# Who spreads k over two heads: from three ScalarE reads to one, and a 0/1 factor on VectorE

## The chip, the cores and the metric

One NeuronCore of one Trainium2 chip runs the whole kernel. The metric is the device time of one launch in microseconds. Before the change it is 622.71 us, the median of 3 runs (622.13 to 622.75).

## The reference

A transformer layer with adaptive normalisation, on x of shape 8 x 512 x 256 (batch, tokens, channels), fp32. With six rows of modulation per batch it computes

```
h = layernorm(x) * (1 + ca) + sa
x = x + ga * attention_block(h)     # 16 heads of 16 channels, causal band of 128 keys,
                                    # then an MLP 256 -> 1024 -> 256 with gelu
h = layernorm(x) * (1 + cb) + sb
x = x + gb * channel_mix(h)         # token shift, receptance, squared relu
```

Inside the attention block, `q = h @ Wq + bq`, `k = h @ Wk + bk`, `v = h @ Wv + bv`, `softmax(q k^T / 4 + band) v`, and an output projection. What is changed here is only how the projected k, with its bias, reaches the layout in which the scores are computed.

## The kernel before

Every engine has its own hand-written order of calls; semaphores join them. The work of attention is cut into 16 units: unit `u` is one batch (`u // 2`) and one half of the heads (8 heads, 128 channels on the 128 partitions). Each unit runs through

- `project(u)` (TensorE): q and k, each [128 channels x 512 tokens], into two of the four PSUM banks of `ring_s`, a ring in which each bank is handed on when its last reader signals. The calls that follow on TensorE are `context(u-2)` (one bank of `ring_s` for the denominators) and then `scores` (two pieces of two matmuls each, one bank a piece). So the second piece of scores takes the bank in which q lay, and waits for its last reader, `s_ql`, and the third piece takes k's.
- `high_qk(u)` (ScalarE) and `low_qk(u)` (VectorE): every value is split into a rounded fp16 part (high) and the fp16 rest (low), because the matmuls run in fp16 and add three products. q goes into `q_two` [128, high/low, 512].
- k goes into `k_two` [128, high/low, 1024]: each token has two adjacent columns, one for the even head of a pair and one for the odd. `pick` [128, 2] holds 1.0 where the partition belongs to that head and 0.0 elsewhere, so in each of the two columns the other head's channels are zero. Column `a` of all tokens is a write with a step of two elements.
- `stacks(u, ...)` (SyncE's queue): DMAs from `q_two` and `k_two` into the layout of `scores`, after `s_ql` and `s_kl`.
- `maxima(u, 0..3)` (TensorE, then VectorE L1527 and L1530): row maxima from the high parts alone; it waits for `s_kh`.

The lines of the profile that matter: L958 is ScalarE's high part of q; L961 its high part of k, once for each column, with scale `pick` and bias `bias_k`; L964 its fp32 copy of k into `kc`. L1513 is VectorE's low part of q from PSUM, L1517 its low part of k from `kc`, once for each column. L983 is ScalarE's copy of the denominators of an earlier unit (`copy_den`), L1480 VectorE's `scale_x`, L1611 `residual_b`, L1562 `residual_a`. On GpSimd, L2174 to L2179 are `select` (the causal band), L2189 and L2191 `sums`, L2218 `scale_y`, L2209 `bias_x`. L342 are the matmuls of `scores`, L361 those of `context`, L307 those of `maxima`. Around `high_qk` ScalarE's order has `copy_den` and `exps` behind it; around `low_qk` VectorE's has `residual_b` (even u from 8) or `scale_x` (odd u) behind it.

In the main part of the kernel a batch, two units, takes 67 us, and its pattern repeats. "Unit 10" is the unit whose q is read at 317 us, "unit 11" the one at 350 us.

Of the kernel before, what the change touches and what calls it, by code (L numbers as in the profile page):

```python
# [8 lines left out]
F16 = mybir.dt.float16  # L9
# [5 lines left out]
P = 128  # L15
# [26 lines left out]
def adaln_block(nc, x, w_attn, w_ff1, w_ff2, w_mix, w_mod, c_t, cols, bo, b2, out):  # L42
# [22 lines left out]
    with ctx:  # L65
# [21 lines left out]
        bias_k = sb("bias_k", [P, 2, 2])  # L87
# [54 lines left out]
        kc = sb("kc", [P, L])  # L142
# [25 lines left out]
        s_qk, s_qh, s_ql, s_kc, s_kh, s_kl = (sem(n) for n in ("qk", "qh", "ql", "kc_s", "kh", "kl"))  # L168
# [21 lines left out]
        s_bm, s_bq, s_cv, s_ro, s_row, s_pick, s_bk = (sem(n) for n in ("bm", "bq_s", "cv_s", "ro", "row_s", "pick_s", "bk"))  # L190
# [17 lines left out]
        squares_v = kc[:, :].rearrange("p (k n) -> p k n", k=KC)  # L208
# [21 lines left out]
        def _(e):  # L230
# [23 lines left out]
            def project(u):  # L254
# [3 lines left out]
                for i in range(2):  # L258
                    c0 = i * D + half * P
                    bank, free = ring_s.take(("qk", u, i), *((s_ql, u + 1), (s_kc, u + 1))[i])  # L260
# [509 lines left out]
            for b in range(3, 7):  # L770
                u = 2 * b
                gp = 8 * b
                scores(gp - 1, 0, 2)
                values(b, 1)
                down(u - 4, 0)
                maxima(u, 3)
                keys(u - 5)
                transposes_b(u - 3)
                max_rows(u)
                scores(gp - 1, 2, 4)  # L780
                project(u + 1)
                context(u - 1)
                scores(gp, 0, 2)
                receptance(u - 5)
                scores(gp, 2, 4)
                scores(gp + 1, 0, 2)
                down(u - 4, 1)
                scores(gp + 1, 2, 4)
                scores(gp + 2, 0, 2)
                values_b(u - 5)  # L790
                up(u - 3, 0, 1)
                maxima(u + 1, 0)
                up(u - 3, 1, 2)
                maxima(u + 1, 1)
                up(u - 3, 2, 3)
                up(u - 3, 3, 4)
                out_project(u - 2)
                maxima(u + 1, 2)
                down(u - 3, 0)
                scores(gp + 2, 2, 4)  # L800
                transposes_d(u - 4)
                scores(gp + 3, 0, 2)
                transposes_a(b + 1)
                down(u - 3, 1)
                maxima(u + 1, 3)
                keys(u - 4)
                scores(gp + 3, 2, 4)
                max_rows(u + 1)
                project(u + 2)
                context(u)  # L810
                scores(gp + 4, 0, 2)
                scores(gp + 4, 2, 4)
                transposes_b(u - 2)
                scores(gp + 5, 0, 2)
                receptance(u - 4)
                maxima(u + 2, 0)
                up(u - 2, 0, 1)
                maxima(u + 2, 1)
                up(u - 2, 1, 2)
                out_project(u - 1)  # L820
                scores(gp + 5, 2, 4)
                scores(gp + 6, 0, 2)
                transposes_d(u - 3)
                scores(gp + 6, 2, 4)
                values_b(u - 4)
                maxima(u + 2, 2)
                up(u - 2, 2, 3)
                up(u - 2, 3, 4)
                values(b + 1, 0)

            scores(NG - 9, 0, 2)
            values(B - 1, 1)
            down(10, 0)
            maxima(NU - 2, 3)
            keys(9)
            transposes_b(11)
            max_rows(NU - 2)
            scores(NG - 9, 2, 4)
            project(NU - 1)
            context(NU - 3)  # L840
            scores(NG - 8, 0, 2)
            scores(NG - 8, 2, 4)
            receptance(9)
            scores(NG - 7, 0, 2)
            scores(NG - 7, 2, 4)
            down(10, 1)
            maxima(NU - 1, 0)
            values_b(9)
            up(11, 0, 1)
            maxima(NU - 1, 1)  # L850
            up(11, 1, 2)
            scores(NG - 6, 0, 2)
            out_project(NU - 4)
            up(11, 2, 3)
            maxima(NU - 1, 2)
            up(11, 3, 4)
            maxima(NU - 1, 3)
            down(11, 0)
            transposes_d(10)
            scores(NG - 6, 2, 4)  # L860
            max_rows(NU - 1)
            down(11, 1)
            scores(NG - 5, 0, 2)
            scores(NG - 5, 2, 4)
            transposes_b(NU - 4)
            receptance(10)
            scores(NG - 4, 0, 2)
            scores(NG - 4, 2, 4)
            keys(10)
            out_project(NU - 3)  # L870
            scores(NG - 3, 0, 2)
            values_b(10)
            scores(NG - 3, 2, 4)
            scores(NG - 2, 0, 2)
            up(NU - 4, 0, 1)
            up(NU - 4, 1, 2)
            context(NU - 2)
            up(NU - 4, 2, 3)
            scores(NG - 2, 2, 4)
            up(NU - 4, 3, 4)  # L880
            scores(NG - 1, 0, 2)
            down(NU - 4, 0)
            transposes_b(NU - 3)
            transposes_d(11)
            scores(NG - 1, 2, 4)
            down(NU - 4, 1)
            up(NU - 3, 0, 1)
            up(NU - 3, 1, 2)
            context(NU - 1)
# [3 lines left out]
            transposes_d(NU - 4)  # L893
            up(NU - 3, 2, 3)
            up(NU - 3, 3, 4)
            out_project(NU - 2)
            down(NU - 3, 0)
            keys(NU - 4)
            down(NU - 3, 1)
            transposes_b(NU - 2)  # L900
            receptance(NU - 4)
            up(NU - 2, 0, 1)
            up(NU - 2, 1, 2)
            out_project(NU - 1)
            up(NU - 2, 2, 3)
            values_b(NU - 4)
            up(NU - 2, 3, 4)
            transposes_b(NU - 1)
            down(NU - 2, 0)
            transposes_d(NU - 3)  # L910
            up(NU - 1, 0, 1)
            down(NU - 2, 1)
            up(NU - 1, 1, 2)
            up(NU - 1, 2, 3)
            keys(NU - 3)
            receptance(NU - 3)
            values_b(NU - 3)
            up(NU - 1, 3, 4)
            transposes_d(NU - 2)
            down(NU - 1, 0)  # L920
            down(NU - 1, 1)
            keys(NU - 2)
            receptance(NU - 2)
            values_b(NU - 2)
            transposes_d(NU - 1)
            warm_end(0, 16)
            keys(NU - 1)
            receptance(NU - 1)
            values_b(NU - 1)

        @block.scalar
        def _(e):
# [14 lines left out]
            def high_qk(u):  # L947
# [3 lines left out]
                if u == 0:  # L951
                    e.wait_ge(s_bk, 2)
# [1540 lines left out]
        def _(e):  # L2493
# [57 lines left out]
            def load_residual(i):  # L2551
# [5 lines left out]
                if i == 1:  # L2557
                    e.wait_ge(s_gates, DMA)
# [218 lines left out]
```

## Time and profile before

| | |
|---|---|
| timed runs | 622.71 us median (622.13 to 622.75) |
| the profiled execution | span 620.5 us from first to last instruction; no further time of its own is recorded |
| TensorE | matmuls busy 567.8 us, 92% |
| ScalarE | busy 446.9 us, 72% |
| VectorE | busy 403.2 us, 65% |
| GpSimd | busy 380.3 us, 61% |
| TensorE's clock | mean granted 0.989 of full speed |

The span is 2.2 us below the median of the timed runs. Times in the rows below count from the span's start. A busy TensorE is not TensorE at its peak; what counts for the change is at which instruction a wait ends last.

### The profile page before, as it was taken

The page shows a single profiled execution, that of the slowest core. Times are in us where ns is not written, and L with a number is a line of the kernel's source. Part 1 is how long each engine was busy: PE and PEld are TensorE (multiplying, and loading weights), DVE is VectorE, ACT ScalarE, POOL GpSimd, SP SyncE. Part 2 cuts the span into 40 slices and gives each one's busy share as a digit, 9 for nine tenths or more (in the row PEclk, how much of TensorE's full clock was granted, in tenths as well). Part 3 has the DMA queues.
Part 4 walks back from the last instruction along what each step waited for, and adds up shares of the span by engine and source line. Part 5 has one row for each costly group of instructions (what it writes and reads, how often), then busy time and mean ns, then how long its engine had stood idle before and what let it go on. Part 6 is the DMA issues. An engine that isn't in the chain of part 4 may idle for free.

```text
span 620.5 us, 16499 instructions
## 1 busy us (share of the span) xinstructions
PE 567.8 (92%) x6528; PEld 444.8 (72%) x6528; DVE 403.2 (65%) x830; ACT 446.9 (72%) x745; POOL 380.3 (61%) x610
## 2 busy tenths in 40 slices
PE   5889988999898999999898989899999989999996
PEld 2668757777776777677667767677767768878785
DVE  4676746686464788576867686578867475375453
ACT  2527447499968777897879786987788798955542
POOL 4387324657937957675767678586657378943430
PEclk9989989899999999999999999999999999999999
DMA  5635423434503051351235132533134242110111
GB/s 176 246 103 133 124 77 78 112 75 116 137 18 101 25 139 52 97 143 56 69 90 153 60 87 76 146 93 89 52 80 112 70 116 52 54 46 26 34 44 35
DMA packets 46364, 55.74 MB, mean 90 GB/s; under 512 B 11643, under 2 KB 33469, under 8 KB 46286
## 3 DMA queue, kind: packets, MB, share of 16 engines
q1 hardware_dynamic: 44454, 53.81, 31.4%
q8 instruction: 52, 0.85, 0.6%
q10 hardware_dynamic: 1832, 0.87, 0.6%
q14 instruction: 26, 0.21, 0.1%
HBM read 22.31 MB, written 4.49 MB: 43 GB/s over the span
## 4 chain that ended last, share of the span: by engine, by line
PE 50%; ACT 17%; DVE 15%; issue 7%; POOL 7%; DMA 1%; SPq 1%; ACTq 1%; DVEq 0%; POOLq 0%
PE rest L486 4%; PE rest L498 4%; PE rest L447 3%; PE rest L449 3%; PE rest L448 3%; DVE nmax L1530 3%; PE quad L342 3%; ACT rest L1048 3%; PE rest L361 3%; PE rest L474 3%; PE rest L239 3%; PE quad L398 2%; ACT hid_hi L1058 2%; ACT p L997 2%; DVE hid_lo L1590 2%
## 5 line engine op out<-in xcount | busy, mean ns | idle before, releaser
L2174 POOL TENSOR_SCALAR_AFFINE_SELECT p<-p 128x448 f32<-128x448 f32 x64 | 41.5, 649 | 102.8 <-ACT p L997 80.5
L1530 DVE TENSOR_REDUCE nmax<-quad 128x8 f32<-128x1032 f32 x64 | 79.0, 1234 | 2.2
L430 PE MATMUL rest<-bt_hi,w_hi 128*128 128x256 f16 x256 | 70.2, 274 | 5.3 <-DVE hid_lo L1590 5.1
L997 ACT ACTIVATE p<-quad,scale_s 128x576 f32<-128x576 f32 (+1 forms) x77 | 62.3, 822 | 15.7 <-PE quad L342 15.4
L1048 ACT ACTIVATE rest<-rest,bias,scale_g 128x256 f32<-128x256 f32 x128 | 63.0, 532 | 11.2 <-PE rest L432 11.0
L447 PE MATMUL rest<-w_hi,hid_hi 128*128 128x256 f16 x256 | 69.9, 273 | 0.9 <-DVE hid_lo L1590 0.9
L432 PE MATMUL rest<-bt_hi,w_lo 128*128 128x256 f16 x256 | 69.8, 273 | 0.0
L431 PE MATMUL rest<-bt_lo,w_hi 128*128 128x256 f16 x256 | 69.8, 273 | 0.0
L449 PE MATMUL rest<-w_hi,hid_lo 128*128 128x256 f16 x256 | 69.8, 272 | 0.0
L448 PE MATMUL rest<-w_lo,hid_hi 128*128 128x256 f16 x256 | 69.8, 272 | 0.0
L1590 DVE SCALAR_TENSOR_TENSOR hid_lo<-rest,inv_f,hid_hi 128x512 f16<-128x512 f32 x64 | 46.8, 744 | 25.1 <-ACT hid_hi L1058 24.8
L2189 POOL TENSOR_TENSOR ps<-p 128x384 f32<-128x384 f32 x56 | 56.7, 1012 | 1.4
L2191 POOL TENSOR_TENSOR ps<-ps,p 128x320 f32<-128x320 f32 x56 | 49.1, 877 | 4.4
L342 PE MATMUL quad<-q_st,k_st 100*128 100x192 f16 (+3 forms) x468 | 45.1, 228 | 6.8 <-DVE x L1562 2.7
L1058 ACT ACTIVATE hid_hi<-rest,inv_f 128x512 f16<-128x512 f32 x64 | 43.4, 687 | 4.5 <-PE rest L449 2.2
L342 PEld LDWEIGHTS quad<-q_st,k_st 100*128 100x128 f16 x468 | 33.1, 97 | 16.7 <-issue 3.7
L1527 DVE COPY_PREDICATED quad<-later,quad 128x248 f32<-128x248 int16 x64 | 26.8, 418 | 28.2 <-PE quad L307 28.1
L361 PE MATMUL rest<-p,v_blk 128*32 128x192 f32 (+2 forms) x1024 | 41.2, 314 | 0.9 <-POOL p L2179 0.9
L361 PEld LDWEIGHTS rest<-p,v_blk 128*32 128x32 f32 x1024 | 31.9, 112 | 12.8 <-issue 5.8
L239 PE MATMUL rest<-ident 128*128 128x128 f32 x292 | 41.1, 292 | 0.0
L239 PEld LDWEIGHTS rest<-ident 128*128 128x128 f32 x292 | 37.1, 202 | 1.8 <-issue 0.7
L1517 DVE SCALAR_TENSOR_TENSOR k_two<-kc,pick,k_two 128x512 f16<-128x512 f32 x32 | 24.7, 827 | 20.1 <-ACT kc L964 20.1
(239 smaller groups left out, 1531.9 us busy)
## 6 DMA issues: line engine op xcount, KB each, us to landing
k_st<-k_two SPq DMA_DIRECT2D x64, 128.0 KB, 2.5
v_blk<-vn SPq DMA_DIRECT2D x16, 512.0 KB, 6.4
q_st<-q_two SPq DMA_DIRECT2D x64, 64.0 KB, 2.6
k_st<-k_two SPq DMA_DIRECT2D x64, 64.0 KB, 2.0
rb<-den_rows SPq DMA_DIRECT2D x16, 256.0 KB
x<-x SPq DMA_DIRECT2D x16, 256.0 KB, 3.0
out<-x SPq DMA_DIRECT2D x16, 256.0 KB, 2.2
xa<-x SPq DMA_DIRECT2D x7, 512.0 KB, 4.8
```

The costliest lines, as they stand in the source:

```text
L239: e.matmul(psum[4 if n < WARM else 7 if n < WARM + 5 else 5][:, 0:P], ident[:, :], ident[:, :], start=True, stop=True)
L342: last = e.matmul(bank[:, c0:c0 + w], k_st[0:MR, half, j, s * P:(s + 1) * P], q_st[0:MR, half, j, s * KW + q0:s * KW + q0 + w], start=True ...
L361: e.matmul(bank[32 * j:32 * j + 32, s * KW:s * KW + w], v_blk[:, s % 2, s // 2, half, 2 * j * HD:2 * (j + 1) * HD], p32[(4 * u + j) % SLOT ...
L430: e.matmul(dst, w1_hi[:, k, ms], bt_hi[:, k, :], start=(k == 0), stop=False)
L431: e.matmul(dst, w1_hi[:, k, ms], bt_lo[:, k, :], start=False, stop=False)
L432: last = e.matmul(dst, w1_lo[:, k, ms], bt_hi[:, k, :], start=False, stop=(k == KC - 1))
L447: e.matmul(dst, hid_hi[:, m, ts], w2_hi[:, m, :], start=(m == 0), stop=False)
L448: e.matmul(dst, hid_hi[:, m, ts], w2_lo[:, m, :], start=False, stop=False)
L449: last = e.matmul(dst, hid_lo[:, m, ts], w2_hi[:, m, :], start=False, stop=(m == MF - 1))
L997: e.activation(p32[gp % SLOTS][:, c0:c0 + 2 * w].rearrange("p (n c) -> p n c", n=2), (rest if gp < APART else quad)[:, b0 % HQ:b0 % HQ + 2 ...
L1048: e.activation(dst, dst, ACT.Gelu_apprx_tanh, bias=bias_1[:, m:m + 1], scale=scale_g[:, 0:1]).then_inc(s_gl, 1)
L1530: e.tensor_reduce(nmax[:, :, :, qt].rearrange("p a j -> p j a"), quad[:, :, 2 * QB - 2:2 * WIN].rearrange("p j (c a) -> p j a c", a=2), AX ...
```

## The change

ScalarE reads the projected k once and writes it rounded to fp16 into the new dense tile `k_one[:, 0, :]`, in place of two scaled reads into `k_two` and one fp32 copy into `kc`. VectorE multiplies that tile by `pick`, once for each column, into the high half of `k_two`; subtracts it from the PSUM value plus bias into `k_one[:, 1, :]`, the low part; does q's low part; and multiplies k's low part by `pick`, twice. `bias_k` and its two small instructions go. The PSUM bank of k is handed on at `s_ko`, after VectorE's read, in place of `s_kc`.

```
 high_qk (ScalarE)
-                    e.wait_ge(s_bk, 2)
+                    e.wait_ge(s_bq, 2)
...
-                kt_hi = k_two[m][:, 0, :]
                 e.activation(q_two[m][:, 0, :], ring_s.at["qk", u, 0][:, :], ACT.Identity, bias=bias_q[:, 2 * m:2 * m + 1]).then_inc(s_qh, 1)
                 e.wait_ge(s_qk, 2 * u + 2)
-                for a in range(2):
-                    e.activation(kt_hi[:, a:2 * L:2], ring_s.at["qk", u, 1][:, :], ACT.Identity, bias=bias_k[:, m, a:a + 1],
-                                 scale=pick[:, a:a + 1]).then_inc(s_kh, 1)
                 hold(e, s_kl, 2 * u)
-                e.activation(kc[:, :], ring_s.at["qk", u, 1][:, :], ACT.Identity, bias=bias_q[:, 2 * m + 1:2 * m + 2]).then_inc(s_kc, 1)
+                e.activation(k_one[:, 0, :], ring_s.at["qk", u, 1][:, :], ACT.Identity, bias=bias_q[:, 2 * m + 1:2 * m + 2]).then_inc(s_kc, 1)
 low_qk (VectorE)
-                e.wait_ge(s_qh, u + 1)
+                if u == 0:
+                    e.wait_ge(s_pick, 1)
+                e.wait_ge(s_kc, u + 1)
+                for a in range(2):
+                    e.tensor_scalar(kt_hi[:, a:2 * L:2], k_one[:, 0, :], pick[:, a:a + 1], None, ALU.mult).then_inc(s_kh, 1)
+                e.scalar_tensor_tensor(out=k_one[:, 1, :], in0=ring_s.at["qk", u, 1][:, :], scalar=bias_q[:, m + 1:m + 2],
+                                       in1=k_one[:, 0, :], op0=ALU.add, op1=ALU.subtract).then_inc(s_ko, 1)
                 e.scalar_tensor_tensor(out=qt_lo[:, :], in0=ring_s.at["qk", u, 0][:, :], scalar=bias_q[:, m:m + 1],
                                        in1=qt_hi[:, :], op0=ALU.add, op1=ALU.subtract).then_inc(s_ql, 1)
-                e.wait_ge(s_kc, u + 1)
+                e.wait_ge(s_ko, u + 1)
                 for a in range(2):
-                    e.scalar_tensor_tensor(out=kt_lo[:, a:2 * L:2], in0=kc[:, :], scalar=pick[:, a:a + 1],
-                                           in1=kt_hi[:, a:2 * L:2], op0=ALU.mult, op1=ALU.subtract).then_inc(s_kl, 1)
+                    e.tensor_scalar(kt_lo[:, a:2 * L:2], k_one[:, 1, :], pick[:, a:a + 1], None, ALU.mult).then_inc(s_kl, 1)
```

The diff has three more kinds of lines. The loops over batches in the five orders are written out call by call; the sequence of calls on every engine is the same as before. Some waits are added: `hold(e, s_xve, n)`, `hold(e, s_hve, n)`, `hold(e, s_bve, i)` and `hold(e, s_cve, i)` ahead of VectorE's four kinds of statistics, each for a small GpSimd instruction of the batch or half batch before, `hold(e, s_h2, 4 * n)` ahead of GpSimd's `rstd_x(n)`, and at one place each `s_hn` and `s_top`. And the scratch of a setup step lies in `h3` instead of `kc`.

## Rows read from the trace of the kernel before

**Rows 1.** The page: busy us of each engine; GpSimd's select (busy, mean ns).

```profile
PE 567.8 (92%) x6528; PEld 444.8 (72%) x6528; DVE 403.2 (65%) x830; ACT 446.9 (72%) x745; POOL 380.3 (61%) x610
...
L2174 POOL TENSOR_SCALAR_AFFINE_SELECT p<-p 128x448 f32<-128x448 f32 x64 | 41.5, 649 | 102.8 <-ACT p L997 80.5
```

**Rows 2.** Chain that ended last, 317 to 352 us: start, us, what.

```profile
317.96 1.68 ACT k_two L961 x2
...
332.10 0.69 DVE x L1562
...
332.84 0.34 PE quad L342 x2
```

**Rows 3.** Waits of TensorE, 230 to 506 us: total us, times, longest.

```profile
PE quad L342 <- DVE x L1562: 2.7, 4, 0.7
```

**Rows 4.** Timeline of ScalarE, units 10 and 11: start, us, line, [idle before].

```profile
317.91 1.74 ACT L961 ACTIVATE k_two<-quad,bias_k,pick 128x512 f16<-128x512 f32 x2
...
319.49 0.68 ACT L964 ACTIVATE kc<-quad,bias_q 128x512 f32<-128x512 f32 x1
...
321.44 0.60 ACT L983 ACTIVATE dn<-quad 128x512 f32<-128x512 f32 x1
...
349.88 0.68 ACT L958 ACTIVATE q_two<-quad,bias_q 128x512 f16<-128x512 f32 x1
...
353.54 0.60 ACT L983 ACTIVATE dn<-quad 128x512 f32<-128x512 f32 x1 [0.83 <-PE quad L381]
```

**Rows 5.** Timeline of VectorE, the same two units.

```profile
320.20 1.68 DVE L1517 SCALAR_TENSOR_TENSOR k_two<-kc,pick,k_two 128x512 f16<-128x512 f32 x2 [1.46 <-ACT kc L964]
...
321.77 0.68 DVE L1611 TENSOR_TENSOR x<-x 128x512 f32<-128x512 f32 x1
...
352.74 1.48 DVE L1517 SCALAR_TENSOR_TENSOR k_two<-kc,pick,k_two 128x512 f16<-128x512 f32 x2 [1.39 <-ACT kc L964]
...
354.12 1.26 DVE L1480 SCALAR_TENSOR_TENSOR h<-xa,mv_x,mod_a 128x256 f32<-128x256 f32 x3
```

**Rows 6.** VectorE's groups by line and shape, whole span.

```profile
L1517 DVE SCALAR_TENSOR_TENSOR k_two<-kc,pick,k_two 128x512 f16<-128x512 f32 x32 | 24.7, 827 | 20.1 <-ACT kc L964 20.1
...
L1513 DVE SCALAR_TENSOR_TENSOR q_two<-quad,bias_q,q_two 128x512 f16<-128x512 f32 x16 | 11.9, 746 | 22.3 <-ACT q_two L958 22.3
...
L1480 DVE SCALAR_TENSOR_TENSOR h<-xa,mv_x,mod_a 128x256 f32<-128x256 f32 x28 | 11.6, 477 | 0.3
```

**Rows 7.** Timeline of GpSimd, the same two units.

```profile
318.47 0.88 POOL L2191 TENSOR_TENSOR ps<-ps,p 128x320 f32<-128x320 f32 x1
...
319.31 1.29 POOL L2218 TENSOR_TENSOR x<-x,mod_g 128x512 f32<-128x512 f32 x1
...
350.67 0.88 POOL L2191 TENSOR_TENSOR ps<-ps,p 128x320 f32<-128x320 f32 x1
...
351.55 1.29 POOL L2209 TENSOR_TENSOR x<-x,row_b 128x512 f32<-128x512 f32 x1
```

**Rows 8.** Timeline, VectorE and GpSimd, at 168 us and at 141 us.

```profile
168.55 0.86 POOL L2191 TENSOR_TENSOR ps<-ps,p 128x320 f32<-128x320 f32 x1
...
169.12 0.84 DVE L1611 TENSOR_TENSOR x<-x 128x512 f32<-128x512 f32 x1
...
169.37 1.05 POOL L2174 TENSOR_SCALAR_AFFINE_SELECT p<-p 128x448 f32<-128x448 f32 x1
...
140.86 2.69 DVE L1489 SCALAR_TENSOR_TENSOR h<-h,rs_x,mod_a 128x256 f32<-128x256 f32 x4
```

**Rows 9.** Timeline of TensorE, the first scores of unit 11.

```profile
353.40 0.50 PE L342 MATMUL quad<-q_st,k_st 100*128 100x192 f16 x4
```

**Rows 10.** Timeline of VectorE, unit 2.

```profile
67.14 0.72 DVE L1513 SCALAR_TENSOR_TENSOR q_two<-quad,bias_q,q_two 128x512 f16<-128x512 f32 x1
...
69.13 0.14 DVE L1693 TENSOR_REDUCE total<-rest 128x1 f32<-128x2 f32 x1
```

**Rows 11.** Waits of TensorE, 107 to 158 us.

```profile
PE quad L342 <- DVE nmax L1530: 0.6, 2, 0.4
```

More of the change, by code:

```diff
@@ new lines, in _ @@
+            values(4, 0)
+            scores(31, 0, 2)
+            values(4, 1)
+            down(4, 0)
+            maxima(8, 3)
+            keys(3)
+            transposes_b(5)
+            max_rows(8)
+            scores(31, 2, 4)
+            project(9)
+            context(7)
+            scores(32, 0, 2)
+            receptance(3)
+            scores(32, 2, 4)
+            scores(33, 0, 2)
+            down(4, 1)
+            scores(33, 2, 4)
+            scores(34, 0, 2)
+            values_b(3)
@@ new lines, in _ @@
+            stats_b(4)
+            output(1)
+            low_a(4)
+            mix(2)
+            maxima(7, 3)
+            add_y(3)
+            low_m(7)
+            low_qk(8)
+            residual_b(3)
+            divide(6)
+            low_b(4)
+            maxima(8, 0)
+            maxima(8, 1)
+            low_f(4, 0, 1)
+            low_f(4, 1, 2)
+            residual_a(5)
+            gated(2)
+            maxima(8, 2)
+            stats_x(5)
+            output(2)
+            stats_b(5)
@@ new lines, in _ @@
+            low_f(4, 2, 3)
+            low_f(4, 3, 4)
+            mix(3)
+            maxima(8, 3)
+            scale_c(6)
+            low_m(8)
+            low_qk(9)
+            scale_x(5)
+            low_b(5)
+            divide(7)
+            shift_x(5)
+            stats_h(5)
+            gated(3)
+            add_y(4)
+            maxima(9, 0)
+            low_f(5, 0, 1)
+            scale_c(7)
+            low_f(5, 1, 2)
+            maxima(9, 1)
+            residual_b(4)
+            residual_a(6)
@@ new lines, in _ @@
+            low_f(5, 2, 3)
+            low_f(5, 3, 4)
+            maxima(9, 2)
+            stats_b(6)
+            output(3)
+            low_a(5)
+            mix(4)
+            maxima(9, 3)
+            add_y(5)
+            low_m(9)
+            low_qk(10)
+            residual_b(5)
+            divide(8)
+            low_b(6)
+            maxima(10, 0)
+            maxima(10, 1)
+            low_f(6, 0, 1)
+            low_f(6, 1, 2)
+            residual_a(7)
+            gated(4)
+            maxima(10, 2)
@@ new lines, in _ @@
+            maxima(11, 1)
+            residual_b(6)
+            residual_a(8)
+            low_f(7, 2, 3)
+            low_f(7, 3, 4)
+            maxima(11, 2)
+            stats_b(8)
+            output(5)
+            low_a(6)
+            mix(6)
+            maxima(11, 3)
+            add_y(7)
+            low_m(11)
+            low_qk(12)
+            residual_b(7)
+            divide(10)
+            low_b(8)
+            maxima(12, 0)
+            maxima(12, 1)
+            low_f(8, 0, 1)
@@ new lines, in _ @@
+            residual_a(15)
+            stats_b(15)
+            low_f(14, 2, 3)
+            gated(12)
+            low_f(14, 3, 4)
+            low_b(15)
+            output(12)
+            mix(13)
+            add_y(14)
+            low_f(15, 0, 1)
+            low_f(15, 1, 2)
+            low_f(15, 2, 3)
+            residual_b(14)
+            gated(13)
+            output(13)
+            low_f(15, 3, 4)
+            mix(14)
+            add_y(15)
+            scale_y(15)
+            residual_b(15)
@@ L2412, in _ @@
+            bias_x(9)
+            select(48)
+            rstd_h(7)
+            bias_h(13)
+            select(49)
+            sums(48)
             scale_y(8)
@@ L2475, in _ @@
[L2475 to L2491 removed]
+            rstd_b(13)
```

1535 lines of the change are left out of this document (966 added, 569 removed).

## The prediction

> **What bounds the kernel now.** I read the page first. TensorE is busy 92% of the span, ScalarE 72%, VectorE 65%, GpSimd 61% [rows 1]. So at most 8% of the span, some 50 us, is there to win, and engine time that is freed elsewhere counts only where a wait of TensorE ends later because of it. Next the chain that ended last: in unit 10 it runs through exactly the work that is changed, ScalarE's two scaled reads of k, then its fp32 copy, VectorE's low parts, `residual_b`, its statistics, the gelu, and `residual_a` (L1562), and comes back to TensorE as a wait of scores [rows 2]. That wait occurs 4 times between 230 and 506 us, 2.7 us in all [rows 3]: units 8, 10, 12 and 14. The odd units between are not on it. Then the timelines of the two units, engine by engine: what stands behind the changed calls, and when TensorE asks.
>
> **ScalarE's side.** Removed: two reads (1.74 us together) and the copy (0.68) [rows 4]; added: one read to dense fp16, by q's own row 0.68. That is 1.7 us of ScalarE per unit, 28 us over 16 units. Most of it shortens no wait. In unit 11, `copy_den` comes next and ScalarE already idles 0.83 us for `context` [rows 4]; in unit 10 two squares follow and then `copy_den` at 321.44, which is when `context` ends too. Finishing earlier makes that idle time longer. I find only units 4 and 5 (119 to 152 us) in which ScalarE goes from the copy straight on for several microseconds. There TensorE's own waits are small: the one for the row maxima that follow is 0.6 us in two times [rows 11]. I take 0.6 us gained; 0 if it is covered again, 3.1 us (two times the 1.55 us by which ScalarE's next call can move up) if all of it comes through.
>
> **VectorE's side.** Before: one q instruction (0.746 us) and two for k (0.827) [rows 6]. After: the same q instruction, one of its shape for k's low part, and four multiplications of a 16-bit tile by a column. Consecutive instructions overlap by 0.11 us (320.20 + 1.68 against 321.77 [rows 5]), so a q-like instruction costs 0.65 us from start to start.
>
> The multiplication is not in this trace: no wide VectorE instruction has one source only, in SBUF, 16 bits wide. Upper end: L1517 with the same strided output, 0.69 us from start to start ((354.12 - 352.74) / 2 [rows 5]). Lower end: two elements a cycle, which would be the 0.39 us of a 256-column instruction ((1.26 - 0.477) / 2 [rows 5, 6]). I take 0.39: every wide row at one element a cycle has a second tensor or a PSUM source, and this has neither. The Trainium skill (VectorE: DVE Perf Modes, section "Mode 2×_2P") says that `tensor_scalar` between SBUF tiles takes two read ports and gives two results a cycle; that would be the low end, and no row here shows it.
>
> Unit 10, by 0.39: the k read runs 317.91 to 318.60, VectorE starts 0.03 later at 318.63 (as 320.17 to 320.20 [rows 4, 5]). Four multiplications and two q-like instructions end at 318.63 + 1.56 + 1.30 = 321.49; the next call started at 321.77. A gain of 0.28 us. By 0.69 it is 322.69, a loss of 0.92. The break-even is 0.46 us a multiplication: VectorE's wait for the copy (1.46 us) used to stand where the new work goes.
>
> **What runs beside them.** GpSimd is in the middle of a row of two-source instructions just when the first two multiplications come: `sums` to 319.35, `scale_y` to 320.60; in unit 11 to 351.55 and 352.84 [rows 7]. Before, VectorE ran q's low part there, which has one SBUF source. At 169.12 a VectorE instruction that reads two SBUF tiles meets a GpSimd one with 0.29 us to go and takes 0.84 us in place of 0.68 (321.77 [rows 5]); the GpSimd instruction behind it takes 1.05 us against a mean of 0.649 [rows 1, 8]. Four more at 140.86 take 2.69 us [rows 8], about 1 us more than L1480's pace. So the two engines do make each other wait, by turns. If a multiplication does so too, the first loses 0.72 - 0.13 = 0.59 us, `scale_y` gets its turn and ends near 320.80, the second loses 1.06, and the next call starts at 323.14: a loss of 1.37 in unit 10. If not, the gain of 0.28 stays. Both ends are open; I take the middle, a loss of 0.55 in each of four units: 2.2 us.
>
> **The bank of q.** This is the new wait. `s_ql` comes behind three more instructions, and the second piece of scores takes that bank. In unit 11 TensorE starts its four matmuls at 353.40 and needs the bank at about 353.6 [rows 9]. ScalarE's k read starts right behind q's (349.88 + 0.68 [rows 4], less 0.10 of overlap: 350.46) and ends at 351.15; VectorE starts at 351.18; q's low part is done at 351.18 + 0.78 + 0.65 + 0.75 = 353.36: 0.2 us to spare. With 0.69 a multiplication it is 353.96, 0.4 us late. With turns: 0.24 lost to `sums`, 1.10 to `bias_x`, done at 354.70, 1.14 us late. The middle of 0 and 1.14 is 0.57, in five odd units (7 to 15): 2.9 us. Nothing takes this back: TensorE is in order, and behind it stand scores, `receptance` and the MLP. VectorE's own next call, 354.12, is hidden by its later wait for TensorE unless it slips by more than 1 us. Even units have more time, since TensorE's `context` starts later against q.
>
> **Unit 2.** Here VectorE comes late and ScalarE has finished: q, k and k took 69.13 - 67.14 = 1.99 us [rows 10]. Now 4 x 0.39 + 2 x 0.65 = 2.86: a loss of 0.9 us, and maxima and `scale_x` behind it are on the chain. With 0.69 it is 2.1.
>
> **Costed at nothing.** `k_two`'s DMAs start later behind other work in SyncE's queue in units 10 and 11 and have idle time behind them. `s_kh` is out before `maxima` asks in both units. The added holds are for GpSimd instructions of the batch or half batch before; uncovered, each would cost the wait for one small instruction. Written-out loops issue the same calls. `bias_k` and the scratch in `h3` touch setup only.
>
> **Sum.** 2.2 + 2.9 + 0.9 - 0.6 = 5.4 us on a span of 620.5, so 625.9; the timed median lies 2.2 us above the span, so 622.7 + 5.4 = 628.1 us.
>
> **Rivals.**
> 1. Each multiplication runs at one element a cycle and waits for nobody. For: it costs what every wide row costs. Against: it has neither of their reasons. 4 x 0.92 + 5 x 0.4 + 2.1 - 0.6 = 7.2: 629.9 us. Chance 0.18.
> 2. They run fast and undisturbed. For: L1517 too reads two SBUF tiles, and its mean is only 0.827 us. Against: [rows 8]. -4 x 0.28 + 0 + 0.9 - 0.6 = -0.8: 621.9 us. Chance 0.21.
> 3. Faster: as 2, and ScalarE's freed time comes through wholly in units 4 and 5, where its calls stand back to back. It decides if TensorE's waits there shrink by more than 1 us. -1.1 + 0.9 - 3.1 = -3.3: 619.4 us. For: ScalarE is the busiest after TensorE. Against: [rows 11]. Chance 0.16.
> 4. Full turns: both multiplications for the high part wait out the whole GpSimd instruction in front, in all nine units. 4 x 1.37 + 5 x 1.14 + 0.9 - 0.6 = 11.5: 634.2 us. For: the row at 169.12. Against: it needs GpSimd to win between two adjacent VectorE instructions each time. Chance 0.10.
>
> The rule beside rival 4 is the Trainium skill's, SBUF — State Buffer, section "Who interferes with whom": VectorE in a two-port mode and GpSimd exclude each other for a whole instruction. By that rule, the trace agrees for instructions with two SBUF sources (0.16 us at 169.12).
>
> My own case, 624 to 632 us, has the remaining 0.35.
>
> **Chances and range.** About 0.2% (1.2 us) is what a measurement here can tell from no change. Faster: rival 3 and a fifth of rival 2, 0.20. Same: the rest of 2, 0.17. Slower: the forecast, rivals 1 and 4, 0.63. The range goes from 620.0, between rivals 2 and 3, to 634.0; outside lie most of rival 3 below and half of rival 4 above, under 0.2. Both signs hold much of the chance, so the forecast's own range is 624 to 632.
>
> **What will show it.** Right: a multiplication of about 0.4 us alone and up to 1.5 us beside `sums`, `scale_y` and `bias_x`; a new wait of L342 for VectorE's `q_two` in odd units; ScalarE busy 28 us less with more idle before L983; and no shorter wait for L1562. Wrong: multiplications at 0.4 us throughout, or at 0.78, or the waits between 107 and 158 us gone. The weakest step is how long the first two multiplications last.

## The result, and the profile after

The changed kernel takes 635.52 us (median of 4 runs, 634.47 to 640.64), the kernel before, timed beside it, 622.73 us (4 runs, 622.13 to 624.51). The ratio is 1.0222, 95% interval 1.0184 to 1.0259: slower by 12.8 us. The forecast was 628.1 us with a range of 620.0 to 634.0, so the sign is right and the time lies outside the range, next to rival 4 (634.2). The profiled execution took 634.47 us with a span of 632.4, which is 11.9 us more than the span before; it is the shortest of the four after, and the one before is a middle one, which is why the spans stand 11.9 apart and the medians 12.8.

The page after, busy us of each engine, against [rows 1]:

```profile
PE 566.7 (90%) x6528; PEld 442.6 (70%) x6528; DVE 427.4 (68%) x876; ACT 423.0 (67%) x713; POOL 382.5 (60%) x610
```

ScalarE has 23.9 us less work (28 were forecast; the durations added up there overlap by about 0.1 us each) and VectorE 24.2 us more. TensorE does the same work in a longer span. VectorE's groups after, by line and shape (busy us, mean ns | idle before and for whom), against [rows 6]:

```profile
L1847 DVE TENSOR_SCALAR k_two<-k_one,pick 128x512 f16<-128x512 f16 x32 | 27.6, 917 | 32.1 <-ACT k_one L1126 32.1
L1854 DVE TENSOR_SCALAR k_two<-k_one,pick 128x512 f16<-128x512 f16 x32 | 15.0, 520 | 0.0
L1850 DVE SCALAR_TENSOR_TENSOR q_two<-quad,bias_q,q_two 128x512 f16<-128x512 f32 x16 | 11.8, 737 | 0.0
L1848 DVE SCALAR_TENSOR_TENSOR k_one<-quad,bias_q,k_one 128x512 f16<-128x512 f32 x16 | 11.7, 732 | 0.0
```

L1847 and L1854 are the same instruction on the same shapes, the first for k's high part, the second for its low part. One takes 917 ns in the mean and the other 520. What differs is what stands beside them. VectorE's timeline of unit 10 (start, us, line, [idle before]), and GpSimd's under it, against [rows 5] and [rows 7]:

```profile
324.54 2.46 DVE L1847 TENSOR_SCALAR k_two<-k_one,pick 128x512 f16<-128x512 f16 x2 [2.22 <-ACT k_one L1126]
326.90 0.73 DVE L1848 SCALAR_TENSOR_TENSOR k_one<-quad,bias_q,k_one 128x512 f16<-128x512 f32 x1
327.55 0.73 DVE L1850 SCALAR_TENSOR_TENSOR q_two<-quad,bias_q,q_two 128x512 f16<-128x512 f32 x1
328.21 0.90 DVE L1854 TENSOR_SCALAR k_two<-k_one,pick 128x512 f16<-128x512 f16 x2
329.00 0.67 DVE L1948 TENSOR_TENSOR x<-x 128x512 f32<-128x512 f32 x1
```

```profile
324.38 0.87 POOL L2614 TENSOR_TENSOR ps<-ps,p 128x320 f32<-128x320 f32 x1
325.20 1.48 POOL L2641 TENSOR_TENSOR x<-x,mod_g 128x512 f32<-128x512 f32 x1
```

The low pair takes 329.00 - 328.21 = 0.79 us from start to start, 0.39 an instruction, the forecast's own figure. The high pair takes 326.90 - 324.54 = 2.36, 1.57 us more, and ends only when `scale_y` has ended at 326.68. That is the full turn of rival 4 (0.59 + 1.06 = 1.65 by the prediction). `scale_y` itself takes 1.48 us in place of 1.29 [rows 7]. In unit 11 the pair takes 2.01 us.

What TensorE makes of it: its waits over the span (us in total, times, longest), against [rows 3]:

```profile
PE quad L341 <- DVE q_two L1850: 8.2, 9, 1.3
...
PE quad L341 <- DVE x L1898: 4.2, 4, 1.0
...
PE quad L302 <- DVE q_two L1850: 2.1, 2, 1.4
...
PE quad L373 <- DVE q_two L1850: 1.3, 1, 1.3
```

The first, third and fourth are new: TensorE waits for the bank of q, which q's low part gives back. The first falls in unit 4 and in units 7 to 14, the third in units 1 and 2, the fourth in unit 5. The second was 2.7 us. The chain of waits in unit 11 (start, us, what), which had nothing of the changed work in an odd unit before:

```profile
357.66 0.70 ACT k_one L1126
...
358.38 2.11 DVE k_two L1847 x2
360.49 0.62 DVE k_one L1848
361.12 0.67 DVE q_two L1850
...
361.83 0.34 PE quad L341 x2
```

**Where the 11.9 us lie.** A useful ruler is the start of ScalarE's read of q in each unit; I call the time to the next unit's start the step of a unit. After minus before, the steps are: unit 4 +1.29, unit 5 +1.34, unit 6 0.0; odd units 7, 9, 11 and 13 +1.21, +0.99, +1.05 and +1.10; even units 8, 10, 12 and 14 +1.29, +1.30, +1.28 and +1.27. Unit 4 itself starts 0.20 earlier (118.22 against 118.42), and from unit 15 to the end it is 137.09 against 137.10. The sum is 2.63 + 4.35 + 5.14 - 0.20, or 11.9 us.

The -0.20 is no sign that units 0 to 3 cost nothing. Up to unit 4, TensorE's mean granted clock is 0.94 in the execution before and 0.97 in the one after. Two runs below that leave this work as it was up to there, e4 and e11, have 0.97 too and start unit 4 at 117.19 and 116.00. The step of unit 2 shows it best (start and end, length, busy us of PE, PEld, DVE, ACT and POOL, granted clock, DMA share, GB/s; before, after, e4, e11):

```profile
63.38:91.58 28.20, 26.74 (x357) 19.96 (x355) 17.13 (x44) 12.63 (x18) 6.92 (x15) 0.88 0.32 89
64.27:91.70 27.43, 25.04 (x357) 19.32 (x355) 18.14 (x47) 11.21 (x16) 6.97 (x15) 0.94 0.37 90
65.25:91.19 25.94, 24.97 (x357) 19.42 (x355) 17.13 (x44) 12.62 (x19) 6.71 (x15) 0.93 0.37 97
62.98:89.18 26.20, 25.07 (x357) 19.35 (x355) 17.12 (x44) 12.61 (x18) 6.72 (x15) 0.93 0.35 96
```

At nearly the same clock the step is 1.2 to 1.5 us longer after the change, and up to unit 4 the loss is 1.0 to 2.2 us. These are single executions, so the size is rough.

### The profile page after: what moved, and what is told of

Read it like the earlier page. It is cut to its first block, busy times and chain, and to the rows that moved or that the text cites. A ratio compares the mean times of both kernels' runs of the same rounds, so it can differ in the third digit from the quotient of the medians.

```text
span 632.4 us, 16579 instructions
## 1 busy us (share of the span) xinstructions
PE 566.7 (90%) x6528; PEld 442.6 (70%) x6528; DVE 427.4 (68%) x876; ACT 423.0 (67%) x713; POOL 382.5 (60%) x610
## 4 chain that ended last, share of the span: by engine, by line
PE 46%; DVE 20%; ACT 15%; POOL 9%; issue 7%; DMA 2%; ACTq 1%; SPq 0%; DVEq 0%; POOLq 0%
PE rest L485 4%; DVE k_two L1847 4%; PE rest L497 4%; PE rest L446 3%; PE rest L448 3%; PE rest L447 3%; ACT rest L1210 3%; DVE nmax L1866 3%; PE quad L341 3%; PE rest L473 3%; ACT p L1159 2%; ACT hid_hi L1220 2%; PE quad L397 2%; PE rest L238 2%; DVE hid_lo L1927 2%
## 5 line engine op out<-in xcount | busy, mean ns | idle before, releaser
L1847 DVE TENSOR_SCALAR k_two<-k_one,pick 128x512 f16<-128x512 f16 x32 | 27.6, 917 | 32.1 <-ACT k_one L1126 32.1
L360 PE MATMUL rest<-p,v_blk 128*32 128x192 f32 (+2 forms) x1024 | 39.8, 307 | 0.9 <-POOL p L2602 0.9
L360 PEld LDWEIGHTS rest<-p,v_blk 128*32 128x32 f32 x1024 | 31.3, 110 | 11.9 <-issue 5.8
```

Of the source, the lines that this page charges most:

```text
L360: e.matmul(bank[32 * j:32 * j + 32, s * KW:s * KW + w], v_blk[:, s % 2, s // 2, half, 2 * j * HD:2 * (j + 1) * HD], p32[(4 * u + j) % SLOT ...
```

## The experiments

This table holds what I read from each timeline; it is worked out, not printed by the profile. "q low" and "block" give, counted from the start of ScalarE's read of q, when q's low part ends and when the last of the unit's k and q instructions on VectorE ends (median of four units). Even is units 8 to 14, odd is 7 to 13; us.

```
kernel          start  step   step   even   odd    q low      block
                of 4   of 4   of 5   step   step   even/odd   even/odd
before          118.42 27.21  35.49  32.68  34.24  1.48 1.47  4.61 4.34
after           118.22 28.50  36.83  33.97  35.33  5.09 4.72  5.91 5.55
e1 q first      117.14 28.26  35.33  33.43  34.24  1.47 1.46  5.39 5.03
e2 hi from PSUM 117.84 29.17  36.49  33.13  34.81  4.25 4.20  5.07 5.01
e3 both         119.99 28.93  35.32  32.75  34.50  1.47 1.47  4.58 4.56
e4 holds only   117.19 27.20  35.49  32.94  34.37  1.47 1.47  4.57 4.36
e5 cut, after   117.10 28.05  36.95  32.97  34.36  4.06 3.70  4.88 4.53
e6 cut, before  116.34 26.76  35.50  32.49  34.49  1.47 1.46  4.41 4.36
e7 q low last   125.47 28.81  37.32  33.43  35.65  5.23 5.04  5.23 5.04
e8 hi late      116.83 27.46  35.57  32.87  34.24  1.47 1.46  4.80 4.46
e12 q second    122.78 28.28  36.19  34.1*  34.66  4.42 4.05  6.04 5.66
* units 10 and 12, see there
```

e4 leaves the k and q work as it was, so its distance from the first row is scatter. Its odd steps are 34.23 to 34.49, against 34.24 to 34.35 before, its even ones 32.22 to 33.22, against 32.28 to 32.76. Differences of 0.3 us in a step, and of more in a single even one, are not results.

**e1: q's low part first.** The kernel after, with one instruction back where it was.

```diff
+    e.wait_ge(s_qh, u + 1)
+    e.scalar_tensor_tensor(out=qt_lo, ...).then_inc(s_ql, 1)
     e.wait_ge(s_kc, u + 1)
     for a in range(2): e.tensor_scalar(kt_hi[:, a:2 * L:2], k_one[:, 0, :], ...)
     e.scalar_tensor_tensor(out=k_one[:, 1, :], ...)
-    e.scalar_tensor_tensor(out=qt_lo, ...).then_inc(s_ql, 1)
```

> The changed kernel with q's low part moved in front of the two multiplications of k's high part, so that q's bank is handed on early; nothing else differs. My theory (two costs: the multiplications wait by turns with GpSimd, and q's bank is handed on late): TensorE's waits of L341 for q_two go from 8.2 us to nearly 0, the multiplications still take up to 1.5 us, and what is left is the 0.8 us that units 8, 10, 12 and 14 lose on the chain plus 0.9 us in unit 2: 626 to 628 us against 635.5 for the changed kernel. Rival A (the 24 us of added VectorE work is the cost, in whatever order): no gain from the order, 634 to 636 us. Rival B (the late bank is the whole cost): 622 to 623 us.

Measured: 626.31 us (624.13 to 631.58, 10 runs), ratio 1.0086 [1.0054, 1.0119]. The new wait for `q_two` is gone, and with it the loss of the odd units (34.24, as before) and of unit 5 (35.33). The even units keep +0.75, and unit 4 keeps +1.05. TensorE's waits between 236 and 520 us in this kernel:

```profile
PE quad L341 <- DVE x L1899: 5.7, 4, 1.5
```

So about 9 of the 13 us hang on the place of one instruction. In the even units, what stays sits in the other path, where the scores wait for `residual_a`. In unit 4 it is the other bank: TensorE waits for the read of k's low part, which now frees k's bank (window 117.14 to 145.40 us).

```profile
PE quad L341 <- DVE k_one L1851: 0.9, 1, 0.9
```

**e2: k's high part from PSUM.** The order of the kernel after, but the multiplication reads the bank and not `k_one`, so it has one source in PSUM.

```diff
-    e.tensor_scalar(kt_hi[:, a:2 * L:2], k_one[:, 0, :], pick[:, a:a + 1], None, ALU.mult)
+    e.tensor_scalar(kt_hi[:, a:2 * L:2], ring_s.at["qk", u, 1], bias_q[:, m + 1:m + 2], pick[:, a:a + 1], ALU.add, ALU.mult)
```

> The changed kernel with the two multiplications of k's high part reading the projected k from PSUM (add bias, times pick, rounded on the way out) instead of the dense SBUF tile; same order. My theory: an instruction that reads PSUM does not wait for GpSimd, so each takes 0.73 to 0.75 us always (now 0.481 to 1.572 us, mean 0.917), GpSimd's scale_y returns to 1.28 us, and per unit the loss falls to 0.3 us on the chain and 0.3 us for the bank, 1.4 us in unit 2: 626 to 628 us. Rival A (added VectorE work is the cost): 32 instructions of 0.74 instead of 0.917 us save 6 us of VectorE's 24, so about a quarter of the loss goes: 632 us. Rival C (the strided 16-bit output makes them slow, not GpSimd): durations stay scattered up to 1.5 us, 635 us.

Measured: 630.92 us (629.61 to 631.41, 4 runs), ratio 1.0141 [1.0107, 1.0175], 3 us above what I expected. The lines of `k_two`'s writers give min/median/max ns; first this kernel, then the kernel after:

```profile
L1847 DVE TENSOR_SCALAR k_two<-quad,bias_q,pick x32: 819/860/882, 27.9 to 492.5; 128x512 f16<-128x512 f32 x32
```

```profile
L1847 DVE TENSOR_SCALAR k_two<-k_one,pick x32: 481/766/1572, 27.9 to 497.5; 128x512 f16<-128x512 f16 x32
L1854 DVE TENSOR_SCALAR k_two<-k_one,pick x32: 494/503/969, 30.1 to 499.6; 128x512 f16<-128x512 f16 x32
```

From PSUM the instruction lasts the same everywhere, with GpSimd beside it or not: the spread of 481 to 1572 ns belongs to the form that reads SBUF. I had put this form at 0.73 to 0.75 us and it is 0.86. q's low part still ends at 4.20 in odd units, and their step is 0.57 longer; units 4 and 5 are 1.96 and 1.00 longer, and the expectation had no term for them.

**e3: both.** q's low part first, then k's high part from PSUM once ScalarE has read the bank.

```diff
+    e.wait_ge(s_qh, u + 1); e.scalar_tensor_tensor(out=qt_lo, ...)
     e.wait_ge(s_kc, u + 1)
-    e.tensor_scalar(kt_hi[:, a:2 * L:2], k_one[:, 0, :], ...)
+    e.tensor_scalar(kt_hi[:, a:2 * L:2], ring_s.at["qk", u, 1], bias_q[:, m + 1:m + 2], ...)
     e.scalar_tensor_tensor(out=k_one[:, 1, :], ...)
-    e.scalar_tensor_tensor(out=qt_lo, ...)
```

> Both edits together: q's low part first, then k's high part from PSUM. My theory: VectorE does q's low part while ScalarE reads k, no turns with GpSimd, so the next VectorE call comes 0.3 us earlier than in the kernel before in units 8, 10, 12 and 14, no wait for q's bank, 1.4 us lost in unit 2: 621 to 624 us, no different from the kernel before or a little faster. Rival A (added VectorE work is the cost): 630 to 633 us.

Measured: 627.01 us (626.67 to 627.43, 4 runs), ratio 1.0081 [1.0049, 1.0113]; a miss. The even steps are back (32.75), and the odd ones nearly: 34.50, a value that odd steps take in e4 and e6 too, where no bank is late. But unit 4 costs 1.72 us more than before: VectorE comes to it late, and k's low part, the last reader of a PSUM bank of the unit, ends 5.42 us after q's read began, where q's low part ended at 3.31 before. TensorE waits for it (window 119.99 to 148.92 us):

```profile
PE quad L341 <- DVE k_one L1852: 1.6, 1, 1.6
```

Another 1.6 us have arisen before unit 4 starts, at a granted clock of 0.96 up to there; what of them is the edit's stays open.

**e4: the added waits alone.** The kernel before, with the added holds and nothing else of the change.

```diff
     e.wait_ge(s_x, DMA * (n + 1))
+    hold(e, s_xve, n)
...
     stats(xa, ...)
...
     e.wait_ge(s_xmv, 4 * (n + 1))
+    hold(e, s_h2, 4 * n)
```

> The kernel before with only the added waits of the change (ahead of VectorE's statistics, GpSimd's rstd_x and one load of SyncE). My theory: they are for work long done, 622.7 us, within 0.2%. Rival D (one of them holds VectorE or GpSimd up and carries part of the 12.8 us): 1 us or more above it.

Measured: 622.43 us (621.03 to 625.08, 10 runs), ratio 1.0011 [0.999, 1.0033]. They cost nothing that can be measured; the interval leaves room for 2 us at most, of the 12.8.

**e5 and e6: GpSimd's neighbours cut short.** In both kernels, after (e5) and before (e6), the multiplication in `scale_y` and the addition in `bias_x` work on 8 of 256 columns. The other columns are left as they are, so this part of the computation is left out. The two are read against each other.

```diff
-    e.tensor_tensor(x1[:, ts, :], x1[:, ts, :], mod_g[:, :]..., ALU.mult)
+    e.tensor_tensor(x1[:, ts, 0:8], x1[:, ts, 0:8], mod_g[:, 0:8]..., ALU.mult)
-    e.tensor_tensor(rows, rows, row_b[:, 1:2, :]..., ALU.add)
+    e.tensor_tensor(rows[:, :, 0:8], rows[:, :, 0:8], row_b[:, 1:2, 0:8]..., ALU.add)
```

> The kernel after with GpSimd's two additions and multiplications of 256 columns a tile, scale_y and bias_x, cut to 8 columns (the other columns are left unscaled, so part of the computation is left out). To be read against the kernel before with the same cut, not against the kernel before itself. If the pair of multiplications is long because the second of them waits out scale_y or bias_x (2.46 us a pair in unit 10, 2.11 in unit 11), the pair falls to some 1.3 us in both, and the two cut kernels stand 12.8 minus 4 x 1.1 minus 5 x 0.9, that is 3 to 5 us, apart. If the loss comes from the order alone (q's low part behind three instructions, its bank released late), the cut changes nothing of it and they stand 11 to 13 us apart.

> The kernel before with the same cut of scale_y and bias_x to 8 columns (part of the computation left out). The mate of the run above. It shortens GpSimd's work, which is off the path that sets the end, and takes waits from VectorE's other instructions: 619 to 622 us by either theory.

Measured: e5 628.35 us (625.38 to 636.21, 9 runs), e6 621.72 us (619.57 to 624.02, 10 runs). They stand 6.6 us apart in place of 12.8 (the profiled spans 5.2). VectorE and GpSimd in unit 10 of e5:

```profile
320.25 1.43 DVE L1847 TENSOR_SCALAR k_two<-k_one,pick 128x512 f16<-128x512 f16 x2 [2.22 <-ACT k_one L1126]
321.58 0.73 DVE L1848 SCALAR_TENSOR_TENSOR k_one<-quad,bias_q,k_one 128x512 f16<-128x512 f32 x1
```

```profile
320.09 0.87 POOL L2614 TENSOR_TENSOR ps<-ps,p 128x320 f32<-128x320 f32 x1
320.92 0.42 POOL L2641 TENSOR_TENSOR x<-x,mod_g 128x16 f32<-128x16 f32 x1
```

The same instructions of VectorE, untouched, take 1.33 us from start to start in place of 2.36, once GpSimd's neighbour is short; nothing else was edited. What is left above 0.79 is the wait for `sums`, 0.54 us. The odd steps fall from +1.09 to nothing (34.36, against 34.49 in e6), although three instructions still stand ahead of q's low part: it ends at 3.70, just in time. So in this kernel neither the order nor the turns cost by themselves in odd units; their sum does. The even steps keep +0.48 against e6, and their block ends 0.47 later. The 6.6 us are more than the 3 to 5 expected. Units 4 and 5, where `scale_y` isn't the neighbour, keep +1.29 and +1.45 (28.05 and 36.95, against 26.76 and 35.50 in e6), and I had not counted them.

**e7: q's low part last, in the kernel before.** No dense k, no multiplication that reads it.

```diff
-    e.wait_ge(s_qh, u + 1); e.scalar_tensor_tensor(out=qt_lo, ...)
     e.wait_ge(s_kc, u + 1)
     for a in range(2): e.scalar_tensor_tensor(out=kt_lo[:, a:2 * L:2], in0=kc, ...)
+    e.wait_ge(s_qh, u + 1); e.scalar_tensor_tensor(out=qt_lo, ...)
```

> The kernel before with one instruction moved: q's low part behind k's two low parts, as late as the change puts it, with no multiplication of the dense k in it. If the late release of q's bank costs by itself (PE's first score matmul of the next unit waits for it), the two low parts ahead of it (1.48 to 1.68 us) put it 1.0 to 1.3 us late in each of nine units: 630 to 634 us. If only the waits by turns with GpSimd cost and the place of q's low part is free: 622 to 624 us. In between, 625 to 629, both count.

Measured: 643.47 us (641.72 to 644.91, 4 runs), ratio 1.0335 [1.0294, 1.0375]: 21 us, far more than expected. I had sized it in nine units. It costs in all: odd steps +1.41, even +0.75, units 4, 5 and 6 +1.6, +1.83 and +1.19, the stretch from unit 15 on +0.75, and unit 4 starts 7.0 us later than before. In units 0 to 3 too q's low part now waits for the fp32 copy, and TensorE waits 2.5 us for it in unit 1; how the 7.0 us divide was not isolated. In odd units this is the bank of q by itself. In even ones the edit also moves the end of the block from 4.61 to 5.23, so there it is both paths. TensorE in unit 11 of e7, start, us, [idle before]:

```profile
369.29 0.34 PE L342 MATMUL quad<-q_st,k_st 100*128 100x192 f16 x2
370.87 0.34 PE L342 MATMUL quad<-q_st,k_st 100*128 100x192 f16 x2 [1.24 <-DVE q_two L1517]
```

**e12: q's low part second, in the kernel after.** Made to test the two paths against each other by a number.

```diff
     for a in range(2): e.tensor_scalar(kt_hi[:, a:2 * L:2], k_one[:, 0, :], ...)
+    e.wait_ge(s_qh, u + 1); e.scalar_tensor_tensor(out=qt_lo, ...)
     e.scalar_tensor_tensor(out=k_one[:, 1, :], ...)
-    e.scalar_tensor_tensor(out=qt_lo, ...)
```

> The kernel after with q's and k's low parts changed about: high multiplications, q's low part, k's low part, low multiplications. Theory of two paths: odd units pay for the end of q's low part beyond 3.65 us after q's high part began (4.70 in the kernel after, so 1.1; here 4.03, so 0.4), even units for the end of the whole block (5.91 against 4.60, so 1.3, here unchanged); units 4 and 5 win at most 0.7 together: 635.5 - 4 x 0.66 - 0.7 = 631 to 633 us. If q's bank sets the even units as well, they win 0.66 each too: 628.5 to 630. If neither, 635.

Measured: 634.33 us (632.51 to 639.33, 6 runs), ratio 1.0202 [1.0165, 1.0239]; three of the runs lie at 632.5 to 633.2, within the 631 to 633 expected, the median 1.3 us above. The steps tell more than the times. Odd: 34.66, +0.42 where +0.4 was expected. Even: units 10 and 12 take 34.02 and 34.17, +1.4. They won nothing although q's low part ends 0.67 us earlier; the block now ends at 6.04 in place of 5.91. (Units 8 and 14 of this execution take 35.82 and 35.27: the granted clock is 0.95 in each, against 1.00 in unit 10.) TensorE's waits in unit 8, the same in unit 10, first of the kernel after, then of e12:

```profile
PE quad L341 <- DVE x L1898: 1.0, 1, 1.0
PE quad L341 <- DVE q_two L1850: 0.8, 1, 0.8
```

```profile
PE quad L341 <- DVE x L1899: 1.8, 1, 1.8
...
PE quad L341 <- DVE k_one L1851: 0.3, 1, 0.3
```

The wait for q's bank goes away and the wait for `residual_a` grows by what it gave: 1.8 us in both.

**e8: both PSUM readers first, the multiplications after them.**

```diff
+    e.wait_ge(s_qh, u + 1); e.scalar_tensor_tensor(out=qt_lo, ...)
     e.wait_ge(s_kc, u + 1)
+    e.scalar_tensor_tensor(out=k_one[:, 1, :], ...)
     for a in range(2): e.tensor_scalar(kt_hi[:, a:2 * L:2], k_one[:, 0, :], ...)
-    e.scalar_tensor_tensor(out=k_one[:, 1, :], ...)
-    e.scalar_tensor_tensor(out=qt_lo, ...)
```

> The kernel after with both low parts that read PSUM (q's, then k's) ahead of the four multiplications, so that both banks go free early and the first multiplications begin some 1.46 us after q's high part, when GpSimd's sums have ended and scale_y or bias_x nears its end. If what the change costs is the banks and the turns, this order pays little: 622 to 626 us, and the first pair of multiplications takes under 1.5 us. If k's high parts are what the scores wait for in each unit, they come later than in the order with q's low part first and it costs more than that one's 626.3: 628 to 632 us.

Measured: 624.72 us (620.43 to 631.53, 10 runs), ratio 1.0041 [1.0006, 1.0076]. Of the orders of these six instructions the best, and still not ahead of the kernel before. Steps, within the scatter of e4: unit 4 +0.25, even +0.19, odd 0. But the first pair did not come in under 1.5 us:

```profile
318.62 1.98 DVE L1852 TENSOR_SCALAR k_two<-k_one,pick 128x512 f16<-128x512 f16 x2
320.49 0.90 DVE L1855 TENSOR_SCALAR k_two<-k_one,pick 128x512 f16<-128x512 f16 x2
```

```profile
318.60 1.28 POOL L2642 TENSOR_TENSOR x<-x,mod_g 128x512 f32<-128x512 f32 x1
```

It meets `scale_y` head on, 0.02 us behind it, and waits it out. So the turn is still paid. What is different is that no reader of PSUM stands behind the pair, and the block ends at 4.80 in place of 5.91.

**e9 to e11: `residual_b` earlier.** In e8's chain of unit 10 the low multiplications (until 321.39) are followed by `residual_b`, its statistics and so on to the scores at 332.34. So e9 puts `residual_b` between the high and the low multiplications in units 8, 10, 12 and 14, e10 ahead of both, and e11 does e10's move in the kernel before. The call of `residual_b` behind `low_qk` goes in return.

```diff
     e.scalar_tensor_tensor(out=k_one[:, 1, :], ...)
+    if u in (8, 10, 12, 14): residual_b(u - 5)      # e10; in e9 behind the kt_hi loop
     for a in range(2): e.tensor_scalar(kt_hi[:, a:2 * L:2], ...)
```

> The order of e8 (both low parts from PSUM first, then the multiplications), and in units 8, 10, 12 and 14 residual_b with its statistics is put between the high and the low multiplications. The chain of waits of e8 runs in unit 10 from the low multiplications (until 321.39) over x, its statistics, GpSimd's rstd and ScalarE's nrm_c to residual_a and the scores at 332.34, so residual_b 0.8 us earlier takes up to 0.8 us off each of the four: 619 to 622 us if that chain sets the even units' end. If the loss sat only in q's bank and the turns, the move pays nothing: 624 to 626.

> As e9, with residual_b ahead of the high multiplications too, as soon as scale_y has ended (3.3 us after q's high part began, against 4.5 in the kernel before). Chain theory: 618 to 622 us, no worse than e9 unless the high and low parts of k, now ready 6.8 us after q's high part, come late for their DMAs at 7.6: then 623 to 627.

> The kernel before with that same move alone: residual_b ahead of k's low parts in units 8, 10, 12 and 14. It tells what of a gain in e10 belongs to the move and what to the dense k. Chain theory: residual_b up to 1.1 us earlier, of which PE's wait for x of 0.67 us a batch can be had: 618 to 621 us. If the move pays nothing, 621.5 to 623.

Measured: e9 625.39 us, ratio 1.0045 [1.0024, 1.0066]; e10 624.88 us, 1.0028 [1.0, 1.0056]; e11 622.60 us, 0.9999 [0.9979, 1.002] (11, 12 and 12 runs). All miss the gain that the chain promised. TensorE's wait for `x` falls (e10: 1.5 us in 4 times against 3.5 in e8), and the medians of the even steps stay where they were (33.03, 32.66 and 32.87 against 32.87 in e8 and 32.68 before). One by one they tell more: units 8, 10, 12 and 14 take 33.45, 32.91, 32.41 and 31.95 in e10, and 33.17, 32.80, 32.94 and 32.45 in e8. A gain of 0.5 us each is there in units 12 and 14. In units 8 and 10 another wait takes its place, for VectorE's low part of the row maxima (230 to 520 us of e10; in e8 it is 0.3 us):

```profile
PE quad L266 <- DVE m_t L1876: 1.9, 2, 1.1
```

The same wait stands in e9, e11 and, 1.3 us in units 10 and 12, in e4, so it is not the work of the move alone. In e10 the block of k and q ends at 6.62, 0.7 us later than in the kernel after, and the even steps don't lose. So what costs in the even units is not that k's parts come late, but that `residual_b` stands behind them.

They also show the scatter of the start. e8, e9 and e10 have the same instructions up to unit 7, and unit 4 starts at 116.83, 121.03 and 121.51 us. The stretch of 60 to 80 us in e8, then in e10 (start and end, length, busy us of PE, PEld, DVE, ACT and POOL, granted clock, DMA share, GB/s):

```profile
60.00:80.00 20.00, 17.46 (x275) 14.17 (x277) 15.07 (x36) 8.07 (x14) 8.76 (x15) 1.00 0.43 110
```

```profile
60.00:80.00 20.00, 16.79 (x189) 13.71 (x192) 13.01 (x31) 7.85 (x13) 5.28 (x12) 0.86 0.42 105
```

The granted clock differs there between executions of the same instructions (e10 has got less far in these 20 us): 1.00, the upper of its two levels (2.4 GHz), against 0.86, a stretch spent partly at the lower (1.2 GHz). The step of unit 2 alone is 26.00 us in e8, at a clock of 1.00, and 31.56 in e10, at 0.84. Differences of medians under some 2 us between kernels of 10 runs are therefore better read from the steps of units 4 to 14, and a start of unit 4 only beside the granted clock up to it.

## Why the prediction was wrong

**Right: the pace of the multiplication.** Taken as 0.39 us from start to start, measured 0.39. **Right: the place of the losses in the steady part**: q's bank in odd units, the block's end and `residual_a` in even ones. e1 takes the odd loss away wholly and leaves 0.75 of the even 1.29. e12 shrinks the odd loss from 1.09 to 0.42 with q's low part 0.67 us earlier, and leaves the even one. The numbers fall on one line: the odd loss is the end of q's low part less 3.63 us (4.72: 1.09; 4.20: 0.57; 4.05: 0.42; 5.04: 1.41; 3.70: nothing clear of e6), the even loss is the end of the block less 4.61 (5.91: 1.29; 5.39: 0.75; 5.07: 0.45; 6.04: 1.4; 4.80: 0.2). In the even units e7 lies off it, 0.75 at 5.23, and so do e9 to e11, whose `residual_b` no longer stands behind the block. **Right: the holds**, by e4.

**Wrong: "Both ends are open; I take the middle"**, in both paragraphs that price the high pair. The even units were put at 0.55 each, the middle of -0.28 and 1.37, and the odd at 0.57, the middle of 0 and 1.14. Measured are 1.29 and 1.09 each, close to the full turn both times. These two terms came to 2.2 + 2.9 and are 5.14 + 4.35: of the 6.5 us between the 5.4 forecast and the 11.9 measured, 4.4 lie here (3.2 more in units 4 and 5, and -1.1 before them). The middle was hardly a possible outcome: the pair is the same form beside the same GpSimd instructions in every steady unit, so it pays its turn in all or in none. e5 (1.03 us less when the neighbour is cut) shows that it pays, and e2 (819 to 882 ns from PSUM, whatever stands beside it) that this belongs to the form that reads SBUF. The row at 169.12 [rows 8] had shown turns for two SBUF sources. The objection to rival 4, that GpSimd would have to win between two adjacent VectorE instructions each time, was no objection: `scale_y` or `bias_x` begins 0.2 to 0.3 us ahead of the second multiplication in each of units 7 to 14, and that one takes 1.53 to 1.57 us every time. In hindsight rival 4's 0.10 was too little.

The Trainium skill (SBUF — State Buffer, section "Who interferes with whom") says that whichever of the two engines issues first holds the shared ports for its whole instruction and the other is blocked. By that rule, this case's trace agrees: 2.36 us for the pair beside `sums` and `scale_y`, 0.79 for such a pair alone. It speaks of any VectorE instruction in a two-port mode, and its order of issue gives the full turns here: in unit 10 `scale_y` begins at 325.20, ahead of the second multiplication, whose record begins at 325.47.

**Wrong: units 4 and 5 as a place of gain.** I took -0.6 there, from ScalarE's relief, and it is +2.63. I had looked for q's bank in units 7 to 15 alone, and for k's, whose last reader moved from ScalarE to VectorE, nowhere. In unit 4 VectorE comes 2.55 us after q's read began, q's low part ends at 4.75 in place of 3.31, without any turn, and TensorE waits 1.3 us for it. With q's bank free early (e1) the wait for k's bank, 0.9 us, takes its place; with both free early (e8) the step is within 0.25 of the one before. In unit 5 turns with `sums` add to it, q's low part ends at 4.60 in place of 1.47, and e1 takes all of that loss away. The freed ScalarE time shows as idle: before `dn` it is 1.70 us in unit 10, where none was, and 2.40 in unit 11, where it was 0.83 [rows 4]. No kernel here isolates a gain from it; e8, with this relief and the banks free early, is not faster than before in any steady step by more than the scatter.

**Wrong by a little, or open.** Unit 15 was counted among the odd units at 0.57 and cost nothing. In unit 2 VectorE's block did get 0.9 us longer (from 67.68 to 70.67, 2.99 us against 2.10 before), as forecast. Unit 4 starts 0.2 us earlier than before, but at a higher granted clock: against e4 and e11, at the same 0.97, it starts 1.0 to 2.2 us later, and TensorE has new waits for `q_two` of 0.7 and 1.4 us in units 1 and 2. So the term of 0.9 was there, rather larger, with a part in unit 1 that was not counted. Rival 4's 11.5 us met the measured 11.9 in part by luck: it lacks 3.2 us in units 4 and 5, and has too much in unit 15 (1.1) and in the size of the turns (0.6); the last 1.1, its 0.9 in units 0 to 3 against -0.2, goes with the clocks of the two executions.

## What to carry to other kernels

Before an instruction is put ahead of a reader of PSUM, ask when TensorE wants that bank: here the place of one VectorE instruction of 0.73 us was worth 9 us of 13. Ask it for every bank whose last reader the change moves, and in every kind of unit, the first ones too. Where a cost depends on a condition that either holds or does not (do these two engines exclude each other here?), price both and give chances; the middle of the two is a value that neither gives. And engine time freed on ScalarE, 24 us here, is worth nothing until a wait of TensorE is named that ends sooner for it.

## What the runs showed of the hardware

- A strided fp16 multiplication by a column (128x512, one SBUF source, output step 2) takes 0.50 us alone and 0.39 from start to start, and up to 1.57 us beside GpSimd's two-source instructions of 0.87 and 1.29 us. Its twin with a PSUM source and an added bias takes 0.86, beside them too.
- Both engines pay: `scale_y` took 1.48 us where it came between the two multiplications of the high pair (unit 10 of the kernel after), in place of 1.29. Where it began 0.02 us ahead of them (e8) it took 1.28, and they waited it out.
- Between two adjacent multiplications, GpSimd's instruction, begun 0.2 to 0.3 us ahead of the second, got its turn in each of units 7 to 14: the second took 1.53 to 1.57 us.
- The granted clock in the first 120 us differs from execution to execution (0.86 to 1.00 in one stretch of 20 us), and with the instructions unchanged unit 4 starts up to 4.7 us later where it is lower (e8, e10).
